# Group norm and attention on one core: four PSUM banks for output tiles in place of two, the statistics on the fourth, and VectorE's order around the second half's softmax

## What is computed

```
xf = group_norm(x, gamma, beta).reshape(B, 1024, 512)
q, k, v = xf @ wq + bq, xf @ wk + bk, xf @ wv + bv
attn = softmax(einsum('bnc,bmc->bnm', q, k) * 512 ** -0.5, axis=-1)
out = einsum('bnm,bmc->bnc', attn, v) @ wp + bp
return out.reshape(B, 32, 32, 512) + x
```

## Time and profile before

| | us |
|---|---|
| median of 3 runs | 2271.57 |
| lowest and highest | 2271.07, 2275.23 |
| span of the profiled execution | 2267.0 |
| TensorE matmul busy | 2190.5 (97%) |
| VectorE busy | 1410.4 (62%) |
| GpSimd busy | 839.1 (37%) |
| ScalarE busy | 670.9 (30%) |

### The profile page before, as it was taken

How to read it: one execution, slowest core, us unless ns; L and a number is a source line. 1 busy time by engine, 2 the same in 40 slices (tenths; PEclk the granted TensorE clock), 3 DMA queues, 4 the chain that set the end, 5 groups by cost and what they waited for, 6 DMA issues and landing times.

```text
span 2267.0 us, 28143 instructions
## 1 busy us (share of the span) xinstructions
PE 2190.5 (97%) x9425; PEld 1783.5 (79%) x9425; DVE 1410.4 (62%) x2280; ACT 670.9 (30%) x1113; POOL 839.1 (37%) x487
## 2 busy tenths in 40 slices
PE   7999999999999999999999999999999999999998
PEld 5878878787787878878788787887878788787886
DVE  6784766837567475675847657375673757747454
ACT  3231423313233141322414223142331323314131
POOL 3343343333434234333433434234332343323433
PEclk9999999999999999999999999999999999999999
DMA  7003021120302103021030211203021030210101
GB/s 162 19 24 89 1 72 39 45 67 0 96 15 56 56 9 93 9 60 51 22 89 0 69 42 36 75 0 89 22 56 56 5 97 9 60 51 15 60 1 56
DMA packets 109259, 106.03 MB, mean 47 GB/s; under 512 B 8492, under 2 KB 74032, under 8 KB 109232
## 3 DMA queue, kind: packets, MB, share of 16 engines
q1 hardware_dynamic: 109184, 105.68, 16.5%
q10 hardware_dynamic: 48, 0.01, 0.0%
HBM read 72.10 MB, written 33.55 MB: 47 GB/s over the span
## 4 chain that ended last, share of the span: by engine, by line
PE 61%; issue 17%; DVE 11%; POOL 7%; ACT 2%; DMA 1%; SPq 1%; POOLq 0%; DVEq 0%; ACTq 0%
PE psum L790 12%; PE psum L792 12%; PE psum L791 12%; PE psum L867 8%; PE psum L868 8%; PE psum L869 8%; DVE score L632 4%; POOL total_part L352 2%; POOL total_part L344 1%; DVE x_t L578 1%; POOL shift L334 1%; ACT v_hi L439 1%; DVE top_part L616 1%; DVE shift L624 1%; DVE total_part L645 1%
## 5 line engine op out<-in xcount | busy, mean ns | idle before, releaser
L867 PE MATMUL psum<-v_hi,pt_hi 128*128 128x512 f32 x1024 | 413.7, 404 | 58.4 <-DVE x_res L657 55.1
L868 PE MATMUL psum<-v_lo,pt_hi 128*128 128x512 f32 x1024 | 409.3, 400 | 0.0
L869 PE MATMUL psum<-v_hi,pt_lo 128*128 128x512 f32 x1024 | 409.1, 400 | 0.0
L790 PE MATMUL psum<-t_hi,xn_hi 128*128 128x512 f32 x1024 | 406.4, 397 | 0.2 <-DVE v_lo L524 0.2
L792 PE MATMUL psum<-t_hi,xn_lo 128*128 128x512 f32 x1024 | 405.0, 396 | 0.0
L791 PE MATMUL psum<-t_lo,xn_hi 128*128 128x512 f32 x1024 | 405.0, 395 | 0.0
L322 POOL TENSOR_TENSOR x_res<-x_res,out_bias 128x512 f32<-128x512 f32 (+1 forms) x144 | 179.4, 1256 | 513.3 <-DVE top_part L616 284.4
L344 POOL TENSOR_TENSOR total_part<-total_part,score 128x512 f32<-128x512 f32 x192 | 308.5, 1607 | 44.9 <-ACT score L456 30.1
L451 ACT ACTIVATE score<-psum 128x512 f32<-128x512 f32 x256 | 151.3, 599 | 481.7 <-PE psum L792 480.4
L616 DVE TENSOR_TENSOR top_part<-top_part,score 128x512 f32<-128x512 f32 x192 | 167.4, 872 | 192.7 <-ACT score L451 190.4
L867 PEld LDWEIGHTS psum<-v_hi,pt_hi 128*128 128x128 f32 x1024 | 199.3, 195 | 111.1 <-DVE x_res L657 64.0
(11 more groups left out here) (101 smaller groups left out, 2988.0 us busy)
## 6 DMA issues: line engine op xcount, KB each, us to landing
x_res<-in_x_dram SPq DMA_DIRECT2D x128, 256.0 KB, 2.8
out_dram<-x_res SPq DMA_DIRECT2D x128, 256.0 KB, 2.1
x_blk<-in_x_dram SPq DMA_DIRECT2D x240, 128.0 KB, 3.0
score<-in_x_dram SPq DMA_DIRECT2D x16, 128.0 KB, 7.7
w_q<-in_L_conv_wq_dram SPq DMA_DIRECT2D x4, 256.0 KB, 4.6
w_k<-in_L_conv_wk_dram SPq DMA_DIRECT2D x4, 256.0 KB, 7.5
w_v<-in_L_conv_wv_dram SPq DMA_DIRECT2D x4, 256.0 KB, 8.1
w_p<-in_L_conv_wp_dram SPq DMA_DIRECT2D x1, 1024.0 KB, 11.2
```

Source lines behind the costliest of these rows:

```text
L790: nc.tensor.matmul(dst, s_hi_, m_hi_, start=n == 0, stop=False)
L867: nc.tensor.matmul(dst, pt_hi[:, m, queries], v_hi[:, m, :], start=m == 0, stop=False)
L868: nc.tensor.matmul(dst, pt_hi[:, m, queries], v_lo[:, m, :], start=False, stop=False)
L869: last = nc.tensor.matmul(dst, pt_lo[:, m, queries], v_hi[:, m, :], start=False, stop=m == NT - 1)
```

## The change

Output tiles use four banks, 4 to 7, so that tile i waits for the drain of tile i - 4. The fourth of them is also the bank of the statistics. TensorE therefore gets two waits: before output tile 3, until VectorE has read the next image's variance out of that bank (`s_pw_in`), and before the first of the statistics matmuls, until the output tiles of the image before are drained (`s_y`). On VectorE `norm` moves behind the last top part, `tile_out(b, 0)` moves ahead of `tile_shift(b, 1)`, tiles 1 to 3 follow the shifts, and the four row parts move behind the `pt_lo` and `t_lo` parts.

```diff
-        o_ps = [psum[:, 4, :], psum[:, 5, :]]
+        o_ps = [psum[:, 4 + i, :] for i in range(TH)]
         stat = psum[:, 7, :]
...
-                nc.vector.scalar_tensor_tensor(out=at, in0=o_ps[i % 2], scalar=total_inv[:, i:i + 1],
+                nc.vector.scalar_tensor_tensor(out=at, in0=o_ps[i % TH], scalar=total_inv[:, i:i + 1],
...
                     if more:
                         if m == 3:
                             variance(b + 1)
-                        if m == 5:
-                            norm(b + 1)
+                if more:
+                    norm(b + 1)
                 totals(b, 0)
                 if more:
                     xn_lo_parts(b + 1)
+                tile_out(b, 0)
                 tile_shift(b, 1)
-                tile_out(b, 0)
                 shifts(b, 1, 0, NT)
-                if more:
-                    for k in range(KC):
-                        row_part(b + 1, k)
-                        if k == 0:
-                            tile_out(b, 1)
-                for i in range(1 if not more else 2, TH):
+                for i in range(1, TH):
                     tile_out(b, i)
                 for j in range(KC):
                     pt_lo_parts(b, 1, 2 * j, 2 * j + 2)
                     if more:
                         split_lo_part(b + 1, "t", 0, j)
+                if more:
+                    for k in range(KC):
+                        row_part(b + 1, k)
                 totals(b, 1)
...
             def group_sum(n, step, rhs):
                 pe.wait_ge(s_stin, n * 2 + step + 1)
+                if step == 0 and not (isinstance(n, int) and n < 2):
+                    pe.wait_ge(s_y, (n - 1) * NT)
...
-            def out_tile(n, i):
+            def out_tile(n, i, more):
...
-                if i > 1 or not starts(n):
-                    pe.wait_ge(s_y, n * NT + max(i - 1, 0))
-                dst = o_ps[i % 2]
+                if i >= TH or not starts(n):
+                    pe.wait_ge(s_y, n * NT + i - TH + 1)
+                if i == TH - 1 and more:
+                    pe.wait_ge(s_pw_in, n + 2)
+                dst = o_ps[i % TH]
```

More of the change, by code:

```diff
@@ L908, in image @@
                 for i in range(TH):
-                    out_tile(b, i)
+                    out_tile(b, i, more)
                 if more:
```

## The result

The changed kernel takes 2182.55 us, the median of four runs (2182.02 to 2183.46), against 2273.4 us for the kernel before in the same measurement (2271.07 to 2276.66). The ratio is 0.960, with a 95% interval of 0.9588 to 0.9612. The forecast was 2185.8 us, in a range of 2181 to 2203.

The account below looks back on a forecast made before the run. TensorE was taken as the bound, idle 55.1 us before output tiles, with slow matmuls behind. Gains 83.2 + 0.8 + 1.8 = 85.8 us off 2267.0 give 2181.2, plus 4.6 outside the span: 2185.8 us, range 2181 to 2203.

Parts of the forecast that it names:

- The main term: Output tiles 0 to 3, images 0 to 14: stages fall to 21.80 us each, idle time and slow matmuls together, 83.2 us.
- Image 0's second stage: Tiles 4 to 7 of image 0: tile 6 no longer waits for the drain of tile 4, gaining 0.8 us.
- The last image: Image 15, stage up to tile 4: 1.8 us gained, while about 2.7 us for pt_lo and its issue stay.
- The term that was mis-sized: Outside the profiled span: 4.6 us added to 2181.2 us, as the median of runs exceeded the span before.
- The walk along VectorE: VectorE's order followed through image 6: drain of tile 0 ends near 980.0, exponentials about 987, pt_lo at 1001.3.
- Exponentials have 2.8 us to spare: Image 6, end of tile 3: exponentials end about 987, TensorE at 989.8, so 2.8 us remain before pt_hi may start.
- 4 us or more: Before output tile 4: pt_lo is ready ahead of TensorE's reads by 4 us or more, so cost 0.
- The new waits and the shared bank: TensorE's two new waits, for the variance and before the statistics: both met on arrival, cost 0, at most 6.6 us.
- GpSimd's idle time: GpSimd ahead of the next image's maximum: idle time falls from 12.4 to about 8 us.
- The slow clock: Rival, 5%: TensorE's stall goes but its slow clock stays; 2216.5 us, or 2201 if half stays.
- The new wait at tile 4: Rival, 7%: TensorE waits on pt_lo before tile 4, slowed by GpSimd's additions; 2216 us, 2246 with slow stretches.
- The third rival: Rival, 2%: another late drain or GpSimd's chain sets the pace, and the time stays within 0.2%.

Follow-up runs that it names:

- e11: The changed kernel measured once more, unaltered, as a yardstick beside later versions: 2183.03 us.
- e2: The changed kernel with VectorE's order of before; four output banks and the two new waits stay: 2194.33 us.
- e7: The changed kernel with nine unread VectorE instructions between the drain of tile 3 and the first pt_lo, in every image: 2186.35 us.
- e3: The changed kernel with three output banks, the statistics alone in bank 7, and without TensorE's two new waits: 2181.02 us.
- e9: The changed kernel with eighteen unread VectorE instructions between the drain of tile 3 and the first pt_lo: 2263.57 us.
- e4: The changed kernel with two output banks and their old waits, VectorE draining tile 0 ahead of xn_lo and tile 1 ahead of the shift: 2221.09 us.
- e1: The changed kernel with two output banks and the old waits again; VectorE's new order stays: 2271.4 us.

## Why the prediction was right

**The main term.** The stage of output tiles 0 to 3: 83.2 us predicted, 83.6 measured. Image 0's second stage: 0.8 and 0.83. That both the idle time and the slow matmuls would go was the step with a rival of its own, and the windows after settle it: 1.00 in every stage. In the profiled execution only the setup and the very end show a lower clock.

**The last image.** 1.8 us predicted; from its tile 0 to the end it took 56.2 us before (2210.79 to 2267.0) and 53.7 after (2127.16 to 2180.9), 2.5 us less. The term was meant for the stretch up to tile 4, and that gave 2.85 us (26.43 to 23.58), for the wait on pt_lo at its end shrank too, from 2.6 to 1.6 us. Tiles 4 to 7 then took about as long as before: 26.28 us with one short wait (0.7 us) and the clock at 0.87, now 26.06 with four short waits (2.9 us together) and the clock at 1.00. In e11, the same kernel, a wait of 2.3 us stood before tile 4, the clock behind it was 0.87 again, and tiles 4 to 7 took 26.15 us. Behind the last matmul 0.7 us were lost.

The setup ended 0.85 us later in this execution. 83.6 + 0.8 + 2.5 - 0.85 = 86.1 us, the whole difference of the spans; the sum said 85.8. That these agree to 0.3 us is in part luck: the last image gave more than predicted, and the setup took as much back.

**The term that was mis-sized** is the last one, "the 4.6 us by which the median of the runs exceeds the profiled span". The changed kernel's profiled execution took 2182.63 us with a span of 2180.9, so what lies around a span is 1.7 us. The other 2.9 us were spread between executions: the kernel before took 2266 to 2282 us from one execution to the next, the changed one 2179.8 to 2183.5. That accounts for nearly all of the 3.3 us between forecast and median.

**The walk along VectorE.** For the part ahead of pt_lo it took the durations from the rows as they were, and missed which instructions now run beside which. The drain of tile 0 ended 12.7 us into the stage (predicted 12.0), since xn_lo took 5.48 us in place of 4.63. GpSimd's reduction of the maximum, which the walk itself had moved 1.7 us earlier, now runs beside xn_lo (944.16 to 946.28), in all fifteen images; in e2, where it starts only behind xn_lo, this takes 4.6 us in each. "Exponentials have 2.8 us to spare" was wrong for image 6: they ended at 957.53, 0.1 us before pt_hi could begin, because the shifts took 7.11 us instead of 4.90. The walk let GpSimd's additions follow the exponentials, 0.6 us earlier than before. They follow its own reduction by some 7 us (6.98, before 7.10), and so began 17.6 us into the stage in place of 19.1, while the shifts begin at 14.1 as before: the two now overlap. It cost nothing, for pt_lo has its own margin. The last pt_lo ended 33.6 us into the stage, predicted 33.3: it began 0.3 us later, and the parts took 10.46 us, predicted 10.5. The margin "4 us or more" is 3.9 us as the trace is read, and a delay of 5.4 us still fits into it (e7), since half of the delay is repaid.

**The new waits and the shared bank**: nothing, as predicted (e3). **GpSimd's idle time**: 8 us predicted, 10.06 measured. Its additions began 1.5 us earlier in the stage, not 0.6, and took 1.9 us less (1.35 and 9.82 us, before 1.70 and 11.41). Of these 3.5 us 0.8 were lost again in the reduction of the sums, which has the row parts beside it now and took 4.09 us in place of 3.25.

**The rivals.** The slow clock went with the stall. The Trainium skill, TensorE: Matmul & The Clock Gate, "A second HAM failure mode: psum-queue depth-cycling", reports a kernel that cycled through PSUM banks with frequent brief idle times of TensorE, and whose clock kept changing. That did not come here: four output banks in turn left no idle time, and the clock was 1.00 in all 15 stages. Brief waits of 0.1 to 2.0 us, which tiles 4 to 7 had in e2 and e4, did not bring the clock down in images 0 to 14 either. The new wait at tile 4 did not come; e2 shows it at 0.9 us an image in the mean once the row parts stand ahead of pt_lo, and e9 shows it at 5.2. The third rival, another late drain, did not come with four banks, but e4 shows that it stood right behind the one removed.

## What to carry to other kernels

When one engine's queue holds both the instruction that frees a buffer and one that waits for something slow, count the tiles that the producer makes during that slow wait: so many banks are needed. Here, with the new order, they are three; reordering for two only uncovered a second slow wait behind the first. Price a stall with the slow matmuls behind it: 55 us idle time cost 86. And a delay put on purpose into the suspected next link measures its margin, which a walk through durations misjudges wherever two engines slow each other.

## What was not expected of the hardware

The same eight shifts beside the same additions of GpSimd take either 4.9 or 7.1 us. Of images 0 to 14 of the changed kernel 8 have the one and 7 the other, with the shifts starting 14.1 us into the stage in all of them; in image 6 of the kernel before, where GpSimd began only after them, they took 4.90. Where the shifts take some 7.1 us, GpSimd's first addition takes 1.28 to 1.35 us; where they take 4.9, it takes 2.06 to 2.67 us, as in image 6 of e1:

```profile
989.36 2.33 POOL L344 TENSOR_TENSOR total_part<-score 128x512 f32<-128x512 f32 x1 [7.18 <-ACT score L456]
```

One side or the other is held. What decides which is not shown: the first addition is recorded 17.59 to 17.70 us into the stage in the 7 images and 17.48 to 18.09 in the 8. The Trainium skill, SBUF — State Buffer, "Who interferes with whom", says that GpSimd and a VectorE instruction with two SBUF inputs contend for a shared pair of ports, which is an exclusive lock. The rows agree: in image 6 of the changed kernel the last two exponentials, each released by one shift, start 1.71 us apart (955.19 and 956.90), where a shift takes 0.6 us alone.

The length of a stall alone does not say whether the clock falls behind it. In the kernel before a stretch at 1.2 GHz followed the stall in 13 of images 0 to 14, behind 2.7 to 4.6 us; in images 0 and 3 none followed 3.64 and 3.17 us. Stalls of 1.74 and 1.18 us left the clock at 1.00 in the nine images of e1 that had them, and in the six with a second stall of some 3.35 us it fell. In e9, stalls of 1.3 to 1.8 us and then 1.6 to 2.1 us were followed by a fall in 5 of 15 images.
